# Weight and row transfers of a fused attention and feed-forward kernel moved to later turns

## The reference

```
x = x + attention16(layernorm(x), ctx, ctx, Wq, Wk, Wv, Wo)     # 16 heads of 16
x = x + ffn(layernorm(x), ...)                                  # 256 -> 1024 -> 256
x = x + gated_attention8(layernorm(x), ctx, ctx, ifgate_w, ...) # 8 heads of 32
x = x + lora_experts(layernorm(x), weight, gate_w, U, V)

def weight_quant_fake(w):                  # both feed-forward weights
    scale = 1.0 / clip(mean(abs(w)), 1e-5)
    return clip(round(w * scale), -1, 1) / scale
```

## Time and profile before

| | us |
|---|---|
| median of 3 runs | 420.19 |
| the three runs | 415.25, 420.19, 420.78 |
| the profiled execution, its own time | 417.46 |
| its span, first to last instruction | 415.7 |

### The profile page before, as it was taken

How to read it: one execution, slowest core, us unless ns; L and a number is a source line. 1 busy time by engine, 2 the same in 40 slices (tenths; PEclk the granted TensorE clock), 3 DMA queues, 4 the chain that set the end, 5 groups by cost and what they waited for, 6 DMA issues and landing times.

```text
span 415.7 us, 9146 instructions
## 1 busy us (share of the span) xinstructions
PE 335.3 (81%) x3086; PEld 237.1 (57%) x3093; DVE 305.9 (74%) x1025; ACT 264.2 (64%) x567; POOL 181.8 (44%) x207
## 2 busy tenths in 40 slices
PE   2999589889999999832877777778488999999864
PEld 2777467667677776610554455446265666666421
DVE  2798645778998988577899999985436777787741
ACT  1565435654545545734798898886668888888520
POOL 1214400211211355128999899982005555445520
PEclk9999989999999999955789999999689999999985
DMA  8399999995463450000000000000001222212000
GB/s 238 124 273 288 322 232 320 251 183 110 84 140 86 113 67 3 1 0 0 2 1 2 0 2 2 2 0 2 0 13 29 39 53 53 52 41 39 26 25 25
DMA packets 43725, 33.68 MB, mean 81 GB/s; under 512 B 19872, under 2 KB 39712, under 8 KB 43552
## 3 DMA queue, kind: packets, MB, share of 16 engines
q1 hardware_dynamic: 43680, 33.11, 32.3%
HBM read 24.71 MB, written 8.39 MB: 80 GB/s over the span
## 4 chain that ended last, share of the span: by engine, by line
PE 49%; DVE 19%; issue 14%; ACT 6%; DMA 4%; POOL 4%; SPq 3%; DVEq 0%; POOLq 0%; ACTq 0%
PE PS L1458 5%; DVE sm L738 4%; PE PS L1235 4%; PE PS L1448 4%; DMA kst<-scr_k 4%; PE PS L1224 4%; PE PS L1214 3%; PE PS L1215 3%; PE PS L1293 3%; PE PS L1254 3%; PE PS L1154 3%; PE PS L1443 3%; PE PS L1421 3%; SPq L315 2%; DVE sm L710 2%
## 5 line engine op out<-in xcount | busy, mean ns | idle before, releaser
L988 ACT ACTIVATE pT<-PS 128x512 f32<-128x512 f32 x64 | 36.6, 596 | 52.5 <-PE PS L1215 52.4
L603 DVE TENSOR_REDUCE negm<-PS 128x4 bf16<-128x512 f32 x64 | 42.3, 684 | 16.5 <-PE PS L1224 16.3
L432 POOL TENSOR_TENSOR sm<-sm,mhalf 128x1 f32<-128x1 f32 x16 | 11.3, 709 | 87.5 <-DVE sm L635 87.5
L448 POOL TENSOR_TENSOR kst<-kst,rows 128x1024 f32<-128x1024 f32 x16 | 37.7, 2356 | 6.4 <-ACT kst L1056 6.2
L1100 ACT ACTIVATE lnT<-PS,Atok 128x128 f32<-128x128 f32 x128 | 36.4, 369 | 3.6 <-PE PS L1399 2.0
L1215 PE MATMUL PS<-identb,negm 128*128 128x128 bf16 x256 | 35.7, 223 | 0.0
L1333 PE MATMUL PS<-identf,w2f 128*128 128x128 f32 x128 | 19.0, 297 | 20.2 <-ACT w2f L1045 20.2
L462 POOL TENSOR_TENSOR kst<-kst,rows 128x1024 f32<-128x1024 f32 x14 | 33.1, 2364 | 0.0
L1235 PE MATMUL PS<-pT,vx 128*32 128x128 f32 x512 | 27.3, 287 | 5.0 <-ACT pT L988 5.0
L1333 PEld LDWEIGHTS PS<-identf,w2f 128*128 128x128 f32 x128 | 15.1, 150 | 24.5 <-ACT w2f L1045 19.2
L1458 PE MATMUL PS<-wd,xT 128*128 128x392 f32 x64 | 27.2, 552 | 1.8 <-DVE rest L882 1.8
(11 more groups left out here) (220 smaller groups left out, 976.2 us busy)
## 6 DMA issues: line engine op xcount, KB each, us to landing
scr_q<-qpart SPq DMA_DIRECT2D x8, 384.0 KB, 4.0
scr_k<-kpart SPq DMA_DIRECT2D x8, 384.0 KB, 5.1
rows<-in_rows SPq DMA_DIRECT2D x1, 2056.0 KB, 9.4
X<-in_x SPq DMA_DIRECT2D x8, 256.0 KB, 4.9
CTXT<-in_ctxT SPq DMA_DIRECT2D x8, 256.0 KB, 4.5
vx<-in_ctx SPq DMA_DIRECT2D x16, 128.0 KB, 3.1
out<-rest SPq DMA_DIRECT2D x16, 128.0 KB, 1.7
qst<-scr_q SPq DMA_DIRECT2D x8, 192.0 KB, 4.7
```

The costliest lines, as they stand in the source:

```text
L448: gp.tensor_tensor(n2[q.slot], n2[q.slot], ln2g, ALU.mult).then_inc(b_g2, 1)
L603: v.tensor_reduce(negm[f.slot % 2][:, 4 * hg:4 * hg + 4], PS[:, 2 + hg % 2, :].rearrange("p (h k) -> p h k", h=4), AX_X, ALU.max, negate=T ...
L988: s.activation(pT[:, hg, :], PS[:, hg % 2, :], ACT.Exp, scale=float(DH0) ** -0.5).then_inc(a_e, 1)
```

## The change

The rows array is loaded in two pieces, and everything but its first piece goes later:

| piece | turn before | turn after |
|---|---|---|
| rows, first 4*D (ln1_g, ln1_b, b2, outnorm; 512 KB) | 2 | 2 |
| rows, the rest (ln2_g, ln2_b, b1, gate bias; 1544 KB) | 2 | 8 |
| w1 | 3 | 5 |
| w2 | 4 | 6 |
| wg, wd, wlv, gcol | 5 | 9 |
| weight_sum on ACT | 3, 4 | 5, 6 |
| sum on PE, weight_means on DVE | 5 | 7 |
| ternary steps on DVE | 6 to 11 | 8 to 13 |
| sum_weights on DVE | 12 | 14 |
| scale_rows on POOL | 12 to 14 | 12 to 14 |

`scale_rows` waits for a new semaphore of the second piece.

```diff
-        ... s_rows = sem("rows_loaded")
+        ... s_rows = sem("first_rows_loaded"); s_rows2 = sem("other_rows_loaded")
                 if part == 0:
-                    sp.dma_start(rows[:], A["rows"].partition_broadcast(128)).then_inc(s_rows, 16)
+                    sp.dma_start(rows[:, 0:4 * D], A["rows"][0:4 * D].partition_broadcast(128)).then_inc(s_rows, 16)
...
+                elif part == 3:
+                    sp.dma_start(rows[:, 4 * D:], A["rows"][4 * D:].partition_broadcast(128)).then_inc(s_rows2, 16)
...
-                if f and isinstance(f.b, int) and 2 <= f.b < 6:
-                    load_weights(f.b - 2)
+                if f and f.b in (2, 5, 6, 8, 9):
+                    load_weights((2, 5, 6, 8, 9).index(f.b))
...
                 row, by = ((b1r, wscale[:, 0:1]), (ln2g, wmean[:, 1:2]), (ln2b, wmean[:, 1:2]))[i]
+                pool.wait_ge(s_rows2, 16)
                 pool.wait_ge(s_wq, 3)
...
-                    if c.b == 3:
+                    if c.b == 5:
                         weight_means()
...
-                if c and 4 <= c.b < 10:
-                    ternary_step(c.b - 4)
-                if c and c.b == 10:
+                if c and 6 <= c.b < 12:
+                    ternary_step(c.b - 6)
+                if c and c.b == 12:
                     sum_weights()
...
-                    if isinstance(f.b, int) and f.b in (3, 4):
-                        weight_sum(f.b - 3)
+                    if f.b in (5, 6):
+                        weight_sum(f.b - 5)
...
-                    if isinstance(c.b, int) and c.b == 3:
+                    if c.b == 5:
                         pe.wait_ge(s_wsum, 2)
```

More of the change, by code:

```diff
@@ L158, in build @@
         s_const = sem("constants_ready"); s_cc = sem("constants_chain")
-        s_wq = sem("weight_means_chain"); s_tq = sem("ternary_chain"); s_sr = sem("rows_scaled"); s_rows = sem("rows_loaded")
+        s_wq = sem("weight_means_chain"); s_tq = sem("ternary_chain"); s_sr = sem("rows_scaled"); s_rows = sem("first_rows_loaded"); s_rows2 = sem("other_rows_loaded")
         s_wsum = sem("weight_sums_ready"); s_wtot = sem("weight_totals_ready")
```

## The result

The changed kernel's median is 415.01 us (412.93 to 416.75, 4 runs), the kernel before in the same measurement 420.49 us. The ratio is 0.990, 95% interval 0.985 to 0.994: faster, by 2.4 to 6.4 us, which is clear of the noise and less than 2%. Two later measurements of the same two kernels gave 0.990 (0.986 to 0.993) and 0.994 (0.991 to 0.996). Over all of them the span of the changed kernel averages 414.35 us (21 executions, standard error 0.4) and that of the kernel before 417.52 us (107 executions, 0.13): 3.2 us less. One more execution of the changed kernel (418.84 us, 1.5% above the fastest of its measurement) was in the slow state and is in no average. The forecast was 417.0 us for the time and 1.46 us for the gain.

A forecast was written before the change was run, and what follows sets the result against it. PE sets the attention turns' 7.50 us pace, with two stack waits behind bulk transfers. Removing 1.46 us, all else at 0, from the four executions' average of 418.4 gave 417.0 us, range 413.7 to 421.2.

The forecast's parts named there:

- Both waits go: Attention turns 3 and 4: PE no longer waits for the stacks of sequences 4 and 5; 1.46 us removed, chance 0.62.
- Rival 3: Attention turns: transfers only change places, stacks of sequences 6 to 10 come late instead; no change, 418.4 us, chance 0.14.
- Rival 4: Stack waits: slower unprofiled runs hold some 3 us more of them, so the median falls to about 414 us; chance 0.12.
- Consumers at nothing: Weight sums on ACT, the wait for the second rows and one more SP issue: all in time, cost 0.
- The excess of 0.96 us: Turn 5, PE waiting for weight means and a late DVE maximum: moves to turn 7 and stays, no gain.
- Ternary steps beside POOL at nothing: Turns 12 and 13, DVE's ternary steps meeting POOL's row scaling: cost 0, at most 4.2 us for both turns.
- Rival 2: Turns 12 and 13: ternary steps held behind POOL's L426, 4.2 us slower, 421.2 us; chance 0.12.
- the room of 0.91: Turns with a ternary step: DVE's yb is ready 0.91 us before PE wants it, so DVE may be that late.
- Volume as the measure of a landing: DMA in attention turns: at most 2.37 MB per 7.50 us turn, 316 GB/s against 332 shown, so no later stack delayed.
- Behind turn 15 all as before, 1.46 us earlier: After the V projection of turn 15: every wait as in the kernel before, only 1.46 us earlier.
- The bounds of 2%: Whole time: 2% (8.4 us) can be told; faster than 411.8 us 0.03, slower than 428.6 us 0.02, within 0.95.

The follow-up runs named there:

- experiment 3: Kernel before with only the consumers (sums, means, ternary steps, sum_weights) two turns later, transfers as they were: ratio 1.000 (0.997 to 1.003), span 417.41 us.
- experiment 8: Changed kernel with weight_means behind DVE's first two maxima of turn 7 and the weight sums in PSUM bank 6: ratio 0.992 (0.989 to 0.995).
- experiment 6: Changed kernel with POOL's scale_rows ahead of its addition of b2, so DVE's instructions come in the midst of it: ratio 0.999 (0.997 to 1.001).
- experiment 5: Kernel before with rows whole in turn 2, w1, w2 and last-stage weights in turns 5, 6 and 9, consumers two turns later: ratio 0.995 (0.992 to 0.997).
- the filled kernel: Changed kernel with useless matrix products where PE waits in the first feed-forward turns, to keep its clock up: ratio 0.997 (0.994 to 1.000).

## Why the prediction was right or wrong

- **Both waits go: right.** Turns 3 and 4 are 7.50, stacks land early, w1, w2 and the second rows are there long before they are wanted. Rival 3 (the transfers only change places) did not happen.
- **The size of that term: right within what the profiles can tell, too small for the time.** I took the visible excesses of one profile, 1.46 us, the largest of four (0.65 to 1.46, mean 1.0). Behind them stands the 17.5 us from the issue of rows to the landed stacks: with PE slow in turn 1 or 2 (granted clock 0.74 and 0.81) the wait shrinks, with PE fast it would grow, and the estimate over seven profiles gives 1.3 to 1.7 us. The spans show 3.2 us. That the stack waits account for all of it is not shown; 1.5 to 2 us stay open.
- **The forecast of 417.0 us came close partly by luck.** It was 2 us high for the first four runs (415.01) and within 1 us of the average of all executions (414.35 and about 1.75 outside the span, 416.1). But its base of 418.4 us was 0.9 us too low (417.52 and 1.75 are 419.3) and its gain 1.7 us too small, and the two errors partly cancel.
- **Rival 4 (longer waits in unprofiled runs): half right.** The gain is larger than the profiled waits, but 3 us of longer waits stand in no profile; the three further ones of the old order had smaller ones, with spans (416.5 to 417.3) close to the average of 417.5.
- **Consumers at nothing: right,** by experiment 3. The excess of 0.96 us moved to turn 7, and experiment 8 shows that it was the place of weight_means that made it.
- **Ternary steps beside POOL at nothing: right for this order.** The step took 1.21 us and POOL's 3.91, within the 3.5 to 4.2 named. DVE started 0.03 us ahead in turn 12 and 0.02 us in turn 13 (149.61 against 149.63). Rival 2 had the kind of loss, though not its size: in experiment 6 POOL is first and the gain is lost, by two holds of 1.37 us together. What a step that starts just behind POOL would cost was not tried; one hold of 0.80 us would fit into the room of 0.91.
- **Volume as the measure of a landing: wrong in detail.** The prediction set 316 GB/s against the 332 of one turn. From the issue of rows to the landed stacks it was 225 GB/s in the old order and 188 in experiment 5, and that kernel's stacks came at 75.06 instead of near 71. My first reason named w1 and rows alike; the rows' second piece is enough.
- **"Behind turn 15 all as before, 1.46 us earlier": wrong in the profiled execution,** which gave 1.7 us back at the low clock in two feed-forward turns. In the two others the feed-forward stage is as before.
- **What can be told: better than I thought.** I had put it at 2%; repeating the kernel before gave 1.000 and 0.999, within 0.2 and 0.3%. The bounds of 2% were counted from the median of 420.19 and the forecast from 418.4; from 418.4 on, 411.8 needs 4.5 times the visible waits and not six times.

## What to carry to other kernels

Put bulk transfers that nobody wants yet behind the small ones that somebody waits for: a queue issues in order, and in this kernel stacks of 768 KB landed 17.5 us after the issue of the bulk in front of them, and after 10.1 us with most of it moved away. Where a transfer paces an engine, measure from its issue to the consumer's start, in several profiles: here that time kept to 0.3 us while the visible waits ran from 0.65 to 1.46 us. If you compare where later stages begin, subtract what differs before the change can act; here it was 1.3 of 2.3 us. Before moving vector work, look at what GpSimd does in the new place and who starts first.

## What the hardware did that I had not expected

- A VectorE instruction that starts 0.1 to 0.3 us behind a GpSimd instruction of 2.85 to 2.99 us is held for 0.79 to 0.81 us (0.47 to 1.26 and 1.28 us with two inputs in SBUF; 0.29 to 1.09 us for a tensor_scalar of 128x256), not for the rest of it. In all these cases it ended 1.38 to 1.40 us after the GpSimd instruction had started. Those of experiment 6 that came 2.1 us after that start, with 0.7 us left, were held 0.56 to 0.58 us. The other way round GpSimd's instruction is held 1.06 us by a VectorE instruction of 1.21 us, nearly all of it.
- The 2056 KB broadcast took 9.2 to 11.5 us, and cut to 512 KB still 6.5 to 6.8 us in the changed kernel, about as long as 64 KB stack pieces took beside it (5.2 to 6.6). Per byte it was not slow: the piece of 1544 KB took 8.4 to 8.9 us (178 to 188 GB/s), and w1, 1024 KB that is no broadcast, 5.0 to 8.7 us (120 to 210 GB/s) in the same three profiles.
- A stretch of 36 us at a granted clock of 0.72 (some 20 us at 1.2 GHz, an estimate from that mean) cost nothing that the filled kernel could win back, and one of 9 us at 0.62 (212 to 221 us) cost 1.7 us. PE was busy 17 of the 36 us and 7.4 of the 9.
